# Selective scan in a four-block kernel: VectorE's products with B in pairs of units, GpSimd's two products at the end of a step

## The chip, the cores and the metric

One NeuronCore of a Trainium2 chip runs the whole program. The metric is the device time of one execution in microseconds (us), the median of several runs. All data are float32.

## The reference, cut to what matters

The program applies four blocks to an image tensor of 4 x 96 channels x 64 x 64. The change lies in the last, a selective scan in four directions (k = 0 to 3) over the 4096 pixels of each of 4 images, with 16 states per channel:

```python
def step(h, inp):
    u_t, d_t, B_t, C_t = inp
    h = jnp.exp(d_t[..., None] * A) * h + (d_t * u_t)[..., None] * B_t[:, :, None, :]
    y = jnp.einsum('bkdn,bkn->bkd', h, C_t)
    return (h, y)
_, ys = jax.lax.scan(step, h0, seq)
```

The product in question is `(d_t * u_t) * B_t`: one value of `d*u` per channel and pixel, times one value of B per state and pixel. It is the second summand of the recurrence.

## The kernel before, in words

The scan stage (`selective_scan`) works on **steps**. A step is one chunk of 512 pixels of one direction of one image; 4 images x 4 directions x 8 chunks make 128 steps, numbered n. Each step has 12 **units** (G = 12): 8 channels x 16 states fill the 128 partitions, 512 pixels lie along the free axis. For unit i of a step:

- PE copies delta to the unit's 128 rows with a matmul into one of three PSUM buffers (`replicate`, L1775, `p_da`, DAS = 3). It waits until the scan of unit i-3 has freed its buffer.
- ACT turns it into the decay by an Exp in place (`decay`, L1920).
- SP has brought `d*u`, repeated for the 16 states, by a DMA from a DRAM scratch into one of 8 ring slots in SBUF (`replicate_du`, L1698, `du_rep`, RING = 8). Slot (12 par + i) mod 8 is overwritten when the unit that used it has been multiplied. `par` is n mod 2.
- VectorE multiplies it with B, which lies in PSUM (`times_b`, L2054, `bu`, BUS = 3 buffers). For two units of a step, i = 5 and i = 11 (`ON_POOL`), GpSimd does this from a copy of B in SBUF (`times_b`, L2008, `pool_bu`), and issues it 4 units ahead of its own loop (BU_AHEAD): before its products with C of units 1 and 7.
- VectorE runs the recurrence along the 512 pixels (`scan`, L2069, into `h[:, i]`). Except in the first chunk of a direction (c = 0) it starts from the last state of the step before, read from `h`.
- GpSimd multiplies `h` with C (`times_c`, L2015, `hc`, a ring of 8), and PE sums over the states, three units at a time (`y_triple`, L1783).

Beside this each step carries the preparation of the next steps. It is written out by hand as positions between the units of each engine's loop, and the engines meet by counting semaphores only. What matters here:

- **PE**: `replicate(0)`, y_triple of the last step, `replicate(1)`, `b_mm(n+1)` (L1750), `replicate(2)`, `low_mm` (L1770, L1771), `replicate(3)`, y_triple, `replicate(4)`, `y_whole` (L1796), `replicate(5)`, `dt_mm(n+2)` (L1736), `replicate(6)`, `y_triple(n, 0)`, `replicate(7)`, `replicate(8)`, `c_mm(n+1)` (L1745), `replicate(9)`, `y_triple(n, 1)`, `replicate(10)`, first half of `delta_sum(n+2)` (L1759, L1760), `replicate(11)`, second half (L1762, L1765), and `replicate(0)` of the next step. The first half of `delta_sum` writes the PSUM tile out of which ACT's `c_copy(n+1)` reads, and waits for that copy.
- **ACT**: after `decay(5)` `take_y` (L1931), after `decay(6)` two activations (L1866, L1867), after `decay(7)` L1871, after `decay(8)` L1875 and L1879, after `decay(9)` L1882 and `c_copy(n+1)` (L1916), after `decay(10)` `b_copy(n+1)` (L1909, which waits until GpSimd has done its last product with B of step n), then `decay(11)`, and `decay(0)` of the next step, then two activations of `delta_and_high` (L1889, L1891).
- **GpSimd**: `times_c` in order of units, its two `times_b`, and `delta_u(n+1)` (L1997) before `times_c(2)`.
- **SP**: `replicate_du` of units 8 to 11 of step n, `restack(n+1)` (four DMAs, L1672), `store_du(n+1)` (L1683), `replicate_du` of units 0 to 7 of step n+1; each waits for the product that frees its slot, in this order.
- **VectorE**: `times_b(i+1)`, then `scan(i)`; where i+1 is one of GpSimd's units the product is left out, so two scans stand together. At i = 11 it is the product of unit 0 of the next step, which waits for `b_copy`.

Of the kernel before, what the change touches and what calls it, by code (L numbers as in the profile page):

```python
# [15 lines left out]
ALU = mybir.AluOpType  # L16
# [10 lines left out]
N = 512  # L27
# [1493 lines left out]
def selective_scan(nc, w, X, du_d):  # L1521
    K, S, R, DL = 4, 16, 6, 8
    G = C // DL
# [6 lines left out]
    TRIPLES = G // YT  # L1530
    HCS = 8
    DAS = 3
    BUS = 3
    RING = 8
    ON_POOL = (5, 11)
    BU_AHEAD = 4
    NB = G - len(ON_POOL)
    COLS = N // H
    GRP = [(i % YT) * YJ + i // YT for i in range(G)]
    with ExitStack() as ctx:  # L1540
# [28 lines left out]
        du_rep = sb("l3_du_rep", [128, RING, N])  # L1569
        c_rep = sb("l3_c_rep", [128, 2, N])  # L1570
        bu = sb("l3_bu", [128, BUS, N])
        h = sb("l3_h", [128, G, N])
        hc = sb("l3_hc", [128, HCS, N])
        b_sb = sb("l3_b_sb", [128, N])
        pool_bu = sb("l3_pool_bu", [128, len(ON_POOL), N])
        pick_f = hc[0:C].rearrange("c a n -> c (a n)")[:, 0:Q // DL * 128].rearrange("c (j p) -> c j p", p=128)

        p_da = [ps(f"l3_p_da{i}", [128, N]) for i in range(DAS)]
        p_b = [ps(f"l3_p_b{i}", [128, N]) for i in range(2)]
# [12 lines left out]
        s_dur = [sem(f"l3_du_replicated{i}") for i in range(RING)]  # L1592
        s_c, s_ccp, s_b = sem("l3_c_mm"), sem("l3_c_copied"), sem("l3_b_mm")
        s_rep, s_da, s_bu, s_h, s_hc, s_ymm, s_ysum, s_y = (sem("l3_" + n) for n in (
            "delta_replicated", "da", "bu", "h", "hc", "y_triple", "y_whole", "y_taken"))

        H0, HC0, YMM0, Y0, HI0, LO0, CCP0, DU0, DUS0, BU0, PBU0 = DAS, G, TRIPLES, 2, 1, 1, 1, 1, 16, 2 * NB, 2 * len(ON_POOL)
        weights = [(xp_dt, "xp_dt"), (dt_w, "dt_w_T"), (w_rep, "w_rep"), (pick_f, "pick"),
# [46 lines left out]
        def ring_at(par, i):  # L1645

            return (G * par + i) % RING

        def ring_count(n, par, i):

            return 16 * (G // 4 * (n - par) // (RING // 4) + (G * par + i) // RING) + 16

        def vector_bus(i):

            return sum(j not in ON_POOL for j in range(i))

        def stacked_by(m, par):

# [2 lines left out]
        @block.sync  # L1661
        def _(sp_):
            for dst, src in weights:
                sp_.dma_start(dst[:], w[src]).then_inc(s_w, 16)

            def restack(m, par):

                sp_.wait_ge(s_lo, m + 1 + LO0)
                sp_.nop(nofuse=True)
                for part in range(2):  # L1670
                    for q in range(PARTS):
                        sp_.dma_start(stacked[part * Q:(part + 1) * Q, par, q].bitcast(F32),  # L1672
                                      parts[q * Q:(q + 1) * Q, part].bitcast(F32)).then_inc(s_stack[par], 16)

            def store_du(m, par):

                sp_.wait_ge(s_du, m + 1 + DU0)
                sp_.nop(nofuse=True)
                sp_.wait_ge(s_bu, NB * (m - 1) + BU0)
                sp_.nop(nofuse=True)  # L1680
                sp_.wait_ge(s_pbu, len(ON_POOL) * (m - 1) + PBU0)
                sp_.nop(nofuse=True)
                sp_.dma_start(du_d[par], du[:]).then_inc(s_dus, 16)  # L1683

            def replicate_du(n, par, i):

                if i == 0:
                    sp_.wait_ge(s_dus, 16 * (n + 1) + DUS0)
                    sp_.nop(nofuse=True)
                user, step_of = (i - RING) % G, (i - RING) // G  # L1690
                if user in ON_POOL:
                    sp_.wait_ge(s_pbu, len(ON_POOL) * (n + step_of) + ON_POOL.index(user) + 1 + PBU0)
                else:
                    sp_.wait_ge(s_bu, NB * (n + step_of) + vector_bus(user) + 1 + BU0)
                sp_.nop(nofuse=True)
                src = du_d[par, GRP[i] * DL:(GRP[i] + 1) * DL]
                src = bass.AP(src.tensor, src.offset, [[0, S], [N, DL], [1, N]])
                sp_.dma_start(du_rep[:, ring_at(par, i)], src).then_inc(s_dur[ring_at(par, i)], 16)  # L1698

            def step(n, par, more):  # L1700
                for i in range(RING, G):
                    replicate_du(n, par, i)
                if more:
                    sp_.wait_ge(s_rep, G * n)
                    sp_.nop(nofuse=True)
                    restack(n + 1, 1 - par)
                    store_du(n + 1, 1 - par)
                    for i in range(RING):
                        replicate_du(n + 1, 1 - par, i)

            store_du(0, 0)
            restack(0, 0)
            for i in range(RING):
                replicate_du(0, 0, i)
            step(0, 0, True)
            with sp_.Fori(0, B * STEPS // 2 - 1) as i:
                step(2 * i + 1, 1, True)
                step(2 * i + 2, 0, True)
            step(B * STEPS - 1, 1, False)

        @block.tensor
        def _(pe):
# [24 lines left out]
            def b_mm(m, par, b, k, c):  # L1747
                pe.wait_ge(s_bu, NB * (m - 1) + BU0)
                pe.nop(nofuse=True)
                pe.matmul(p_b[par][:], w_rep[:, k, 0, :], u_of(b, k, c), start=True, stop=True).then_inc(s_b, 1)  # L1750
# [280 lines left out]
        @block.vector  # L2031
        def _(dve):
            dve.wait_ge(s_setup, K)
            dve.tensor_copy(w_dt[:].rearrange("c k d -> c (k d)"), p_bc[0:C, 0:K * C]).then_inc(s_setup_cp, 1)
            dve.wait_ge(s_w, 16 * len(weights))
            dve.tensor_copy(pick[:], pick_f[:]).then_inc(s_setup_cp, 1)
            dve.tensor_scalar(minus[:], ident[:], -1.0, None, ALU.mult).then_inc(s_setup_cp, 1)
            dve.tensor_scalar(minus_r[:], ident[:], -1.0, None, ALU.mult).then_inc(s_setup_cp, 1)
            dve.tensor_reduce(d_sum[:], cols[:, K:2 * K], AX_X, ALU.add).then_inc(s_setup_cp, 1)
            dve.memset(ln_one[:], 1.0).then_inc(s_setup_cp, 1)  # L2040
            dve.wait_ge(s_a, 2)
            dve.tensor_scalar(a_neg[:], a_neg[:], -1.0, None, ALU.mult).then_inc(s_a, 1)
            dve.tensor_scalar(ln_one[:], ln_one[:], -1.0, None, ALU.mult).then_inc(s_a, 1)
            dve.wait_ge(s_setup_cp, 6)
            dve.tensor_scalar(d_diag[:], ident[:], d_sum[:], None, ALU.mult).then_inc(s_setup_cp, 1)
            for s, credit in ((s_bu, BU0), (s_h, H0), (s_dus, DUS0)):
                dve.sem_inc(s, credit)

            def times_b(n, i, par):
                if i == 0:  # L2050
                    dve.wait_ge(s_bcp, n + 1)
                dve.wait_ge(s_dur[ring_at(par, i)], ring_count(n, par, i))
                dve.wait_ge(s_h, G * n + i + 1 - BUS + H0)
                dve.tensor_tensor(bu[:, i % BUS, :], du_rep[:, ring_at(par, i)], p_b[par][:], ALU.mult).then_inc(s_bu, 1)  # L2054

            def scan(n, k, c, i, par):
                backward = k >= 2
                way = slice(None, None, -1) if backward else slice(None)
                first = 0 if backward else N - 1
                dve.wait_ge(s_da, G * n + i + 1)  # L2060
                dve.wait_ge(s_hc, G * (n - 1) + i + 1 + HC0)
                if i in ON_POOL:
                    dve.wait_ge(s_pbu, len(ON_POOL) * n + ON_POOL.index(i) + 1 + PBU0)
                    of = pool_bu[:, ON_POOL.index(i), way]
                else:
                    dve.wait_ge(s_bu, NB * n + vector_bus(i) + 1 + BU0)
                    of = bu[:, i % BUS, way]
                state = 0.0 if isinstance(c, int) and c == 0 else h[:, i, first:first + 1]
                dve.tensor_tensor_scan(h[:, i, way], p_da[i % DAS][:, way], of, state, ALU.mult, ALU.add).then_inc(s_h, 1)  # L2069

            def step(b, n, k, c, par, n1, n2, before):
                for i in range(G):
                    if i < G - 1 and i + 1 not in ON_POOL:
                        times_b(n, i + 1, par)
                    if i == G - 1 and n1:
                        times_b(n + 1, 0, 1 - par)
                    scan(n, k, c, i, par)

            times_b(0, 0, 0)
            all_steps(step)(dve)  # L2080
            dve.wait_ge(s_y, B * STEPS + Y0)

# [201 lines left out]
```

## Time and profile before

| | us |
|---|---|
| median of 3 runs (lowest, highest) | 5742.23 (5741.26, 5752.42) |
| the profiled execution: its own time | 5744.95 |
| its span in the trace | 5743.1 |
| first scan of the scan stage starts | 3070.7 |
| last scan starts | 5653.8 |
| VectorE busy over the span | 4640.4 (81%) |
| PE busy | 4971.3 (87%) |
| GpSimd busy | 3832.2 (67%) |
| ACT busy | 2949.7 (51%) |

The span runs from the first to the last recorded instruction. Busy time is the sum of the records of an engine; on VectorE and ACT the record of an instruction overlaps the start of the next by some 0.09 us when they follow without a gap, so the time that an instruction takes out of a busy engine is read from start to start, not from its record. The scan stage takes 45% of the span, and the change touches only that stage.

### The profile page before, as it was taken

To read this page: it belongs to the slowest core of one execution; us is meant where nothing else is said; L and a number is where in the kernel's file an instruction comes from. 1 tells how busy PE (TensorE), PEld (TensorE's weight loads), DVE (VectorE), ACT (ScalarE), POOL (GpSimd) and SP (SyncE) were. 2 spreads that over 40 slices of the span, in tenths; PEclk is the share of its full clock that TensorE was granted. 3 is DMA by queue.
4 is the path that set the end of the run, shared out by engine and by line. 5 is a ranking of instruction groups with operands and counts; after the bars stand their busy time and mean duration, and the time that the engine had idled before them with its cause. 6 is when DMAs were issued, how large, how long until landed. Compare 5 with 4: busy or idle time off the path is not lost. (4 is left out here: it accounts for less than half of the span.)

```text
span 5743.1 us, 74310 instructions
## 1 busy us (share of the span) xinstructions
PE 4971.3 (87%) x16018; PEld 2207.8 (38%) x16018; DVE 4640.4 (81%) x5047; ACT 2949.7 (51%) x4576; POOL 3832.2 (67%) x2568
## 2 busy tenths in 40 slices
PE   6999889897779999998297888888888888888887
PEld 1222256464256666665152222222222222222222
DVE  4876643434418989899797999999999999999996
ACT  5776544443311111111135777777777777777776
POOL 0000032322418898888786999989998999999993
PEclk9998899998889999998698999999999999999998
DMA  2000000001777787776405667667766666677663
GB/s 47 0 0 0 7 1 1 0 1 56 226 158 139 138 152 140 147 141 107 91 9 138 185 183 189 185 182 189 187 186 178 186 185 187 184 189 189 187 184 100
DMA packets 373418, 711.24 MB, mean 124 GB/s; under 512 B 76604, under 2 KB 111224, under 8 KB 358936
## 3 DMA queue, kind: packets, MB, share of 16 engines
q1 hardware_dynamic: 373144, 708.17, 50.2%
q8 instruction: 100, 1.64, 0.1%
q14 instruction: 174, 1.43, 0.1%
HBM read 575.33 MB, written 82.32 MB: 115 GB/s over the span
## 5 line engine op out<-in xcount | busy, mean ns | idle before, releaser
L2015 POOL TENSOR_TENSOR l_hc<-l_h,l_c_rep 128x512 f32<-128x512 f32 x1536 | 1929.8, 1276 | 216.0 <-DVE l_h L2069 187.1
L2069 DVE TENSOR_TENSOR_SCAN l_h<-l_p_da,l_h,l_bu 128x512 f32<-128x512 f32 x1120 | 1412.8, 1279 | 10.5 <-ACT l_p_da L1920 8.8
L1920 ACT ACTIVATE l_p_da<-l_p_da,l_a_neg 128x512 f32<-128x512 f32 x1536 | 1008.5, 658 | 733.8 <-PE l_p_da L1775 712.9
L1221 POOL TENSOR_TENSOR l2b_prod<-l2b_v,l2b_attn 128x1568 f32<-128x1568 f32 x276 | 937.3, 3461 | 242.9 <-DVE l2b_osum L1269 125.2
L1775 PE MATMUL l_p_da<-l_stacked,l_pick 96*128 96x512 f32 x1536 | 908.9, 593 | 191.3 <-DVE l_h L2069 179.1
L2054 DVE TENSOR_TENSOR l_bu<-l_du_rep,l_p_b 128x512 f32<-128x512 f32 x1280 | 855.7, 669 | 29.7 <-DMA l_du_rep<-du_scratch 22.5
L1775 PEld LDWEIGHTS l_p_da<-l_stacked,l_pick 96*128 96x128 f32 x1536 | 293.7, 192 | 1162.4 <-DVE l_h L2069 900.3
L1269 DVE TENSOR_REDUCE l2b_osum<-l2b_prod 128x32 f32<-128x1568 f32 x384 | 665.7, 1780 | 62.9 <-POOL l2b_prod L1221 59.2
L1783 PE MATMUL l_p_y<-l_hc,l_y_pick 128*32 128x512 f32 x3072 | 566.4, 626 | 74.3 <-POOL l_hc L2015 71.7
L1174 ACT ACTIVATE l2b_logits<-l2b_conv,l2b_this_b 98x512 f32<-98x512 f32 x96 | 66.2, 689 | 870.5 <-PE l2b_conv L1139 870.5
L615 POOL TENSOR_TENSOR l_w_pos_low<-l1a_w_sed,l_w_pos_high 96x1536 fp32r<-96x1536 f32 x1 | 4.1, 4123 | 711.2 <-DVE l_w_fc_high L595 711.2
L1139 PE MATMUL l2b_conv<-l2b_img_high,l2b_w_conv_high 128*98 128x512 f32 x1344 | 358.8, 420 | 38.7 <-DMA l2b_img_low<-qkv_scratch 38.7
L1139 PE MATMUL l2b_conv<-l2b_img_high,l2b_w_conv_low 128*98 128x512 f32 x1344 | 338.8, 403 | 0.0
L1139 PE MATMUL l2b_conv<-l2b_img_low,l2b_w_conv_high 128*98 128x512 f32 x1344 | 337.3, 402 | 0.0
L2008 POOL TENSOR_TENSOR l_pool_bu<-l_du_rep,l_b_sb 128x512 f32<-128x512 f32 x256 | 326.7, 1276 | 0.0
L1139 PEld LDWEIGHTS l2b_conv<-l2b_img_high,l2b_w_conv_high 128*98 128x98 f32 x1344 | 231.7, 174 | 148.4 <-issue 38.1
L2069 DVE TENSOR_TENSOR_SCAN l_h<-l_p_da,l_h,l_pool_bu 128x512 f32<-128x512 f32 x224 | 287.4, 1283 | 1.3 <-ACT l_p_da L1920 1.0
L770 POOL TENSOR_TENSOR l1b_h_h_low<-l1b_h_h,l1b_h_h_high 128x512 fp32r<-128x512 f32 x96 | 125.6, 1320 | 226.2 <-DVE l1b_h_h_high L734 226.2
L1139 PEld LDWEIGHTS l2b_conv<-l2b_img_high,l2b_w_conv_low 128*98 128x98 f32 x1344 | 219.6, 163 | 103.9
L1139 PEld LDWEIGHTS l2b_conv<-l2b_img_low,l2b_w_conv_high 128*98 128x98 f32 x1344 | 219.6, 163 | 102.3
L1759 PE MATMUL l_p_bc<-l_relu_x,l_ident 96*96 96x512 f32 x256 | 144.6, 648 | 66.5 <-ACT l_c_rep L1916 59.3
L2069 DVE TENSOR_TENSOR_SCAN l_h<-l_p_da,l_bu 128x512 f32<-128x512 f32 x160 | 192.6, 1222 | 7.7 <-ACT l_p_da L1920 7.6
(267 smaller groups left out, 8905.2 us busy)
## 6 DMA issues: line engine op xcount, KB each, us to landing
l_du_rep<-du_scratch SPq DMA_DIRECT2D x1536, 256.0 KB, 3.8
l2b_img_high<-qkv_scratch SPq DMA_DIRECT2D x192, 306.2 KB, 5.6
l2b_img_low<-qkv_scratch SPq DMA_DIRECT2D x192, 306.2 KB, 9.4
l_stacked<-l_parts SPq DMA_DIRECT2D x512, 96.0 KB, 2.7
l2b_v<-v_scratch SPq DMA_DIRECT2D x192, 152.0 KB, 6.4
qkv_scratch<-l2a_strip SPq DMA_DIRECT2D x32, 840.0 KB, 5.2
du_scratch<-l_du SPq DMA_DIRECT2D x128, 192.0 KB, 2.1
v_scratch<-l2a_v_strip SPq DMA_DIRECT2D x32, 228.0 KB, 4.2
```

The costliest lines, as they stand in the source:

```text
L770: pool.tensor_tensor(h_hl[1][:, f, :], h[:, f, :], h_hl[0][:, f, :], ALU.subtract).then_inc(s_h_lo, 1)
L1139: mm = pe.matmul(p_conv[n % 2][:], w_conv[w_part][:, g, dx, :], img[x_part][:, b % 2, row:row + 2 * CP - 1:2, dx:dx + W], start=(at == 0), ...
L1221: return eng.tensor_tensor(dst.rearrange("q x (dy dx) -> q x dy dx", dx=WIN), window, attn_half[:, :, unit % 2].rearrange("q x (dy dx) -> ...
L1269: dve.tensor_reduce(osum[:, half, unit // 2, unit % 2, :], prod[which][:], AX_X, ALU.add).then_inc(s_sum, 1)
L1759: pe.matmul(p_bc[0:C, :], ident[:], relu_x[:], start=True, stop=False)
L1775: pe.matmul(p_da[i % DAS][:], pick[:, GRP[i] % (Q // DL), :], stacked[:, par, GRP[i] * DL // Q, :], start=True, stop=True).then_inc(s_rep, 1)
L1783: mm = pe.matmul(p_y[par][q * 32:(q + 1) * 32, :], y_pick[:, t, :], hc[:, (G * par + YT * t + q) % HCS, :], start=(t == 0), stop=False)
L1920: act.activation(p_da[i % DAS][:], p_da[i % DAS][:], ACT.Exp, scale=a_neg[:, k * G + GRP[i]:k * G + GRP[i] + 1]).then_inc(s_da, 1)
L2008: pool.tensor_tensor(pool_bu[:, at, :], du_rep[:, ring_at(par, i)], b_sb[:], ALU.mult).then_inc(s_pbu, 1)
L2015: pool.tensor_tensor(hc[:, (G * par + i) % HCS, :], h[:, i, :], c_rep[:, par, :], ALU.mult).then_inc(s_hc, 1)
L2054: dve.tensor_tensor(bu[:, i % BUS, :], du_rep[:, ring_at(par, i)], p_b[par][:], ALU.mult).then_inc(s_bu, 1)
L2069: dve.tensor_tensor_scan(h[:, i, way], p_da[i % DAS][:, way], of, state, ALU.mult, ALU.add).then_inc(s_h, 1)
```

## The change

VectorE's ten products with B of a step become five instructions, each for two units next to each other (0 and 1, 2 and 3, up to 8 and 9). An instruction reads two ring slots of `du_rep` (1024 elements), reads B's 512 columns of PSUM twice by a step of zero, and writes two of now four `bu` buffers. It waits for the DMAs of both units. GpSimd's two units are now 10 and 11 instead of 5 and 11. VectorE's loop changes its order: `scan(i)` comes first, behind it, for even i up to 6, the pair (i+2, i+3), and behind `scan(10)` the pair (0, 1) of the next step. So a step's order is scan 0, pair (2, 3), scan 1, scan 2, pair (4, 5), scan 3, scan 4, pair (6, 7), scan 5, scan 6, pair (8, 9), scan 7, scan 8, scan 9, scan 10, pair (0, 1) of n+1, scan 11. GpSimd issues its two products before its products with C of units 6 and 7. SP's waits for a free ring slot now count pairs.

```diff
-    BUS = 3
+    BUS = 4
-    ON_POOL = (5, 11)
+    ON_POOL = (10, 11)
-    NB = G - len(ON_POOL)
+    NB = (G - len(ON_POOL)) // 2
...
+        def bu_at(par, i):
+            return (2 * NB * par + i) % BUS
...
-                    sp_.wait_ge(s_bu, NB * (n + step_of) + vector_bus(user) + 1 + BU0)
+                    sp_.wait_ge(s_bu, NB * (n + step_of) + user // 2 + 1 + BU0)
...
             def times_b(n, i, par):
                 if i == 0:
                     dve.wait_ge(s_bcp, n + 1)
-                dve.wait_ge(s_dur[ring_at(par, i)], ring_count(n, par, i))
-                dve.wait_ge(s_h, G * n + i + 1 - BUS + H0)
-                dve.tensor_tensor(bu[:, i % BUS, :], du_rep[:, ring_at(par, i)], p_b[par][:], ALU.mult).then_inc(s_bu, 1)
+                for j in (i, i + 1):
+                    dve.wait_ge(s_dur[ring_at(par, j)], ring_count(n, par, j))
+                user = i + 1 - BUS if i >= BUS else i + 1 + 2 * NB - BUS - G
+                if user >= 0 or not (isinstance(n, int) and n == 0):
+                    dve.wait_ge(s_h, G * n + user + 1 + H0)
+                both = p_b[par][:]
+                both = bass.AP(both.tensor, both.offset, [list(both.ap)[0], [0, 2], [1, N]])
+                at = bu_at(par, i)
+                dve.tensor_tensor(bu[:, at:at + 2, :], du_rep[:, ring_at(par, i):ring_at(par, i) + 2, :],
+                                  both, ALU.mult).then_inc(s_bu, 1)
...
-                    dve.wait_ge(s_bu, NB * n + vector_bus(i) + 1 + BU0)
-                    of = bu[:, i % BUS, way]
+                    dve.wait_ge(s_bu, NB * n + i // 2 + 1 + BU0)
+                    of = bu[:, bu_at(par, i), way]
...
             def step(b, n, k, c, par, n1, n2, before):
                 for i in range(G):
-                    if i < G - 1 and i + 1 not in ON_POOL:
-                        times_b(n, i + 1, par)
-                    if i == G - 1 and n1:
+                    scan(n, k, c, i, par)
+                    if i % 2 == 0 and i + 2 < 2 * NB:
+                        times_b(n, i + 2, par)
+                    if i == G - 2 and n1:
                         times_b(n + 1, 0, 1 - par)
-                    scan(n, k, c, i, par)
```

## Rows read from the trace of the kernel before

**Rows 1.** Page, costliest groups: busy us, mean ns | idle before, releaser.
```profile
L2015 POOL TENSOR_TENSOR l_hc<-l_h,l_c_rep 128x512 f32<-128x512 f32 x1536 | 1929.8, 1276 | 216.0 <-DVE l_h L2069 187.1
L2069 DVE TENSOR_TENSOR_SCAN l_h<-l_p_da,l_h,l_bu 128x512 f32<-128x512 f32 x1120 | 1412.8, 1279 | 10.5 <-ACT l_p_da L1920 8.8
...
L2054 DVE TENSOR_TENSOR l_bu<-l_du_rep,l_p_b 128x512 f32<-128x512 f32 x1280 | 855.7, 669 | 29.7 <-DMA l_du_rep<-du_scratch 22.5
```

**Rows 2.** Windows: busy (x) of PE, PEld, DVE, ACT, POOL, clock, DMA share, GB/s.
```profile
4000.00:4500.00 500.00, 435.38 (x1354) 142.64 (x1353) 490.98 (x541) 357.52 (x597) 457.16 (x368) 0.98 0.69 184
```

**Rows 3.** VectorE's timeline, one step from its scan 0 (4953.73) to the next: start, duration.
```profile
4953.73 1.30 DVE L2069 TENSOR_TENSOR_SCAN l_h<-l_p_da,l_h,l_bu 128x512 f32<-128x512 f32 x1
4954.92 0.68 DVE L2054 TENSOR_TENSOR l_bu<-l_du_rep,l_p_b 128x512 f32<-128x512 f32 x1
4955.50 1.30 DVE L2069 TENSOR_TENSOR_SCAN l_h<-l_p_da,l_h,l_bu 128x512 f32<-128x512 f32 x1
...
4961.99 1.30 DVE L2069 TENSOR_TENSOR_SCAN l_h<-l_p_da,l_h,l_pool_bu 128x512 f32<-128x512 f32 x1
...
4973.80 1.29 DVE L2069 TENSOR_TENSOR_SCAN l_h<-l_p_da,l_h,l_bu 128x512 f32<-128x512 f32 x1
```

**Rows 4.** VectorE's timeline in a first chunk (c = 0).
```profile
4533.44 1.23 DVE L2069 TENSOR_TENSOR_SCAN l_h<-l_p_da,l_bu 128x512 f32<-128x512 f32 x1
4534.57 0.67 DVE L2054 TENSOR_TENSOR l_bu<-l_du_rep,l_p_b 128x512 f32<-128x512 f32 x1
```

**Rows 5.** VectorE's groups by form, other blocks: larger element-wise products and sums.
```profile
L1221 DVE TENSOR_TENSOR l2b_prod<-l2b_p_v,l2b_attn 128x1568 f32<-128x1568 f32 x108 | 191.8, 1776 | 0.7
...
L345 DVE TENSOR_TENSOR l_dt<-l_gain 96x1024 f32<-96x1024 f32 x32 | 38.7, 1211 | 0.0
...
L347 DVE TENSOR_TENSOR l_gain<-l_dt 96x512 f32<-96x512 f32 x32 | 22.0, 687 | 1.1
```

**Rows 6.** PE's timeline, the same step as rows 3 (L1775: units 4, 8, 0 of the next).
```profile
4956.85 0.50 PE L1775 MATMUL l_p_da<-l_stacked,l_pick 96*128 96x512 f32 x1 [0.24 <-DVE l_h L2069]
...
4963.35 0.50 PE L1775 MATMUL l_p_da<-l_stacked,l_pick 96*128 96x512 f32 x1 [0.40 <-DVE l_h L2069]
...
4967.77 1.07 PE L1759 MATMUL l_p_bc<-l_relu_x,l_ident 96*96 96x512 f32 x2 [0.38 <-ACT l_c_rep L1916]
...
4971.08 0.80 PE L1775 MATMUL l_p_da<-l_stacked,l_pick 96*128 96x512 f32 x1
```

**Rows 7.** ACT's timeline, the same step (L1920: units 4, 8, 0 of the next).
```profile
4957.39 0.66 ACT L1920 ACTIVATE l_p_da<-l_p_da,l_a_neg 128x512 f32<-128x512 f32 x1 [0.56 <-PE l_p_da L1775]
...
4964.09 0.64 ACT L1920 ACTIVATE l_p_da<-l_p_da,l_a_neg 128x512 f32<-128x512 f32 x1
...
4971.91 0.66 ACT L1920 ACTIVATE l_p_da<-l_p_da,l_a_neg 128x512 f32<-128x512 f32 x1 [1.29 <-PE l_p_da L1775]
```

**Rows 8.** Two scans that waited for their decay: ACT's and VectorE's timelines.
```profile
4549.03 0.66 ACT L1920 ACTIVATE l_p_da<-l_p_da,l_a_neg 128x512 f32<-128x512 f32 x1 [1.39 <-PE l_p_da L1775]
...
4549.90 1.23 DVE L2069 TENSOR_TENSOR_SCAN l_h<-l_p_da,l_pool_bu 128x512 f32<-128x512 f32 x1 [0.44 <-ACT l_p_da L1920]
...
5173.98 0.66 ACT L1920 ACTIVATE l_p_da<-l_p_da,l_a_neg 128x512 f32<-128x512 f32 x1 [1.29 <-PE l_p_da L1775]
...
5174.67 1.22 DVE L2069 TENSOR_TENSOR_SCAN l_h<-l_p_da,l_bu 128x512 f32<-128x512 f32 x1
```

**Rows 9.** Who waited for the decay tile l_p_da: us in all, times.
```profile
  DVE l_h L2069: 20.9, 17
```

**Rows 10.** GpSimd's timeline, the same step as rows 3.
```profile
4955.19 1.28 POOL L2015 TENSOR_TENSOR l_hc<-l_h,l_c_rep 128x512 f32<-128x512 f32 x1 [0.51 <-DVE l_h L2069]
4956.44 1.27 POOL L2008 TENSOR_TENSOR l_pool_bu<-l_du_rep,l_b_sb 128x512 f32<-128x512 f32 x1
```

**Rows 11.** The DMA queue's timeline of that step, and issue to landing of l_du_rep.
```profile
4963.29 11.21 SPq L1698 DMA_DIRECT2D l_du_rep<-du_scratch  x10
...
DMA to landing us min/median/max: 3.0/3.8/6.8
```

More of the change, by code:

```diff
@@ L1647, in ring_at @@
             return (G * par + i) % RING
+        def bu_at(par, i):
+            return (2 * NB * par + i) % BUS
         def ring_count(n, par, i):
             return 16 * (G // 4 * (n - par) // (RING // 4) + (G * par + i) // RING) + 16
-        def vector_bus(i):
-            return sum(j not in ON_POOL for j in range(i))
         def stacked_by(m, par):
```

## The prediction

> **What bounds the kernel now.** I read the costliest groups first [rows 1]: in the scan stage VectorE runs 1536 scans (the row has 1120 of them) of 1.28 us and 1280 products of 0.67 us, and both groups have next to no idle time before them. The stage's windows come next [rows 2]: of 500 us VectorE is busy 491, PE 435, GpSimd 457, ACT 358. So VectorE ends the stage, but PE and GpSimd have little to spare. Then one step on VectorE [rows 3]: from product to scan it is 0.58 us, from scan to the next instruction 1.19 us, start to start. The step holds ten products and twelve scans, 10 x 0.58 + 12 x 1.19 = 20.08 us, and the row shows 4973.80 - 4953.73 = 20.07. There is no gap in it. In a first chunk a scan takes 1.13 [rows 4], so such a step would need 5.80 + 13.56 = 19.36. There are 16 first chunks and 112 others.
>
> **The pairs, on VectorE alone.** A step loses ten products of 0.58 and gets five of 1024 elements. No row shows a product that reads PSUM twice by a step of zero. Nearest are element-wise rows of other blocks [rows 5]: 512 elements 687 ns, 1024 elements 1211 ns, so 512 more elements cost 0.524; and a product out of PSUM with a windowed pattern, 1568 elements in 1776 ns, against 669 for 512 [rows 1], which is 1.048 ns per element, 0.537 for 512. A pair then takes 0.58 + 0.524 to 0.537 = 1.104 to 1.117 start to start; by its whole record less the usual overlap of 0.09 it would be 1.12. I take 1.115, nearest to the row that reads PSUM. Two singles are 1.16, so a pair saves 0.045 us (0.04 to 0.056), a step 0.225, the stage 128 x 0.225 = 28.8 us (25.6 to 35.8). The new order puts no scan and no pair right behind the instruction whose result it needs, so I add nothing for that; five added waits for DMAs are taken by the sequencer while the engine works, at nothing as the old ones are now. What remains of the saving depends on who is late next.
>
> The Trainium skill (Vector Engine (DVE) Microarchitecture Reference, section on the rate slope and fixed cost) gives 1.0417 ns per column plus about 75 ns per instruction after overlap; the trace has 0.58 - 0.533 = 0.045 us here, so it does not agree in size. By the page the saving would be an estimated 128 x 5 x 0.075 = 48 us.
>
> **The chain behind VectorE.** The scan of unit i needs its decay, that needs PE's replicate, and that needs the scan of i-3. Between them PE and ACT do the preparation. The tight place is around the step's end. Scan 5 starts at 4961.99 [rows 3]; replicate(8) starts 1.36 later at 4963.35 [rows 6]. From a replicate to its decay, where ACT is free, it is 4957.39 - 4956.85 = 0.54 [rows 6, 7]. From decay(8) at 4964.09 to decay(0) of the next step at 4971.91 it is 7.82 [rows 7]: ACT runs its activations without a gap up to c_copy, which releases PE's L1759 [rows 6], and four delta_sum products and two replicates follow on PE without a gap. From the start of a decay to the scan that waits for it the trace has 0.87 and 0.69 [rows 8]. Today scan 0 starts 4973.80 - 4971.91 = 1.89 after its decay, so it has 1.02 us to spare.
>
> After the change more of VectorE's work stands ahead of scan 5 and less behind it. Scan 5 starts 5 x 1.19 + 3 x 1.115 = 9.30 us into the step (now 8.26). Behind it VectorE alone has 7 x 1.19 + 2 x 1.115 = 10.56 us to the next scan 0; the chain has 1.36 + 0.54 + 7.82 + 0.69 to 0.87 = 10.41 to 10.59. So **VectorE alone gives a step of 19.86, the chain 19.71 to 19.89**: a tie. I take 19.87, a gain of 0.205, and 112 such steps give 23.0 us. In a first chunk scan 5 starts at 5 x 1.13 + 3 x 1.115 = 9.00, its record is 0.06 shorter, and the chain ends at 9.00 + 10.35 to 10.53 = 19.35 to 19.53, against 19.14 for VectorE and 19.36 now: 16 steps lose 0 to 0.17, I take 1.6 us in all.
>
> **What the lost slack costs.** Today a scan waits for its decay 17 times, 20.9 us in all [rows 9]. The granted clock in the stage averages 0.98 [rows 2], so for a small part of it PE runs at the lower of its two levels, 1.2 instead of 2.4 GHz, and a step in which this meets the chain starts up to 1.02 us late without a trace today. With no slack left each of the 17 waits can grow by 1.0 (17 us), and hidden ones show; some shrink, since early delays on ACT now end before decay(8). Between 0 and 17 I take 8.
>
> **Edits that I cost at nothing, and their cover.** GpSimd: product follows product by 1.25 us [rows 10], so its 15 operations of a step take 18.6 of 19.9. Its product for unit 5 no longer stands ahead of times_c(1). Counted on from scan 5 (times_c follows a scan's start by 4955.19 - 4953.73 = 1.46 us where it waits [rows 3, 10]), it does times_c(5) at 10.8, the product for 10 at 12.0, times_c(6) at 13.2, the product for 11 at 14.5 to 15.8. VectorE needs the first at scan 10, at 16.4, the second at 18.7. ACT's b_copy waits for the second and would run 15.9 to 16.5; decay(11) behind it waits for PE until some 17.0 anyway, and the pair (0, 1) of the next step needs b_copy at 17.6. Both have about 1 us. SP: the ten issues before the next step's need take 11.21 us and land in 3.8 (6.8 at most) [rows 11]. The slots of the pair (0, 1) are written from 9.6 us into the step and now are both needed at 17.6 (unit 0 at 19.5 before), land at 14 to 17; replicate_du(10) waits for the whole pair (2, 3), some 1.2 us into the step plus 1.1, and restack behind it moves by up to 1 us, of the 10 that it is early. ACT's other decays keep 0.7 us (unit 11) or more. Nothing here ends last, but all of it is closer.
>
> **Sum.** -23.0 + 1.6 + 8 = -13.4 us. The profiled execution took 5744.95, so 5731.6 against its own time; the median of the runs is 2.7 lower, 5742.23 - 13.4 = **5729 us**. 0.2% is 11.5 us, about what a measurement of this kernel can tell from no change: faster means below 5730.7, slower above 5753.7.
>
> **Rivals.**
> 1. VectorE alone counts: the wake-up is 0.69 in most steps, delays stay rare, or the pair is cheaper than the rows say. For it: nearly every step of rows 3's kind has no gap. Against it: the chain ends within 0.03 us of VectorE's own. With the full 28.8 us the time is 5713, with 0.056 saved by a pair 5706. Chance 0.18.
> 2. The part of a product that does not grow with its length is larger than the rows say, and a pair saves 0.075 us, taking 1.085. VectorE alone would then need 14.28 + 5.43 = 19.71 per step, the chain 5.95 + 3.26 + 10.41 to 10.59 = 19.62 to 19.80. Steps of 19.71 to 19.80 gain 0.27 to 0.36 each, 35 to 46 us; less 8 for the delays that is 5704 to 5715. Against it: 0.58 start to start for 512 elements leaves no such part. Chance 0.04. (The fixed cost of the page named above is this case.)
> 3. The chain holds the stage: a link is 0.15 us longer than I read it, at PE (L1759 right behind replicate(10), which now starts near 14.1 us) or ACT. Each 0.1 us costs 12.8 us; 0.15 with the delays gives -13.4 + 19 = 5748, within 0.2%. For it: there is no slack to absorb a link. Against it: all links are taken from one gapless stretch. With the gain merely halved by delays (17 us instead of 8) it is 5738. Chance of the group 0.22.
> 4. **Slower**: GpSimd's late second product. It decides from the point where the product for unit 11 ends over 1.0 us later than counted (16.8 us into the step instead of 15.8): then b_copy is late, the pair (0, 1) waits, and decay(11) and delta_sum's results queue behind b_copy on ACT. Each 0.1 us beyond it costs 12.8 us; 0.3 beyond it, with the gain of 13 gone as well from the lengthened step (20.17), gives 5742 + 12 + 8 = 5762. For it: both products now lie between times_c(5) and times_c(7), in the busiest part of GpSimd's step. Against it: GpSimd still stands idle for 0.51 us at the step's start [rows 10], so it catches up there. Chance 0.07.
>
> **How the numbers follow.** My forecast (5717 to 5738) has 0.49, the four rivals 0.18, 0.04, 0.22 and 0.07. Faster by over 0.2% are rivals 1 and 2 and about six tenths of the forecast's range, since 5730.7 cuts it just above its middle: 0.53. Same: the rest of it and rival 3: 0.40. Slower: 0.07. The range goes from 5708 (near rival 1 with 0.056 saved by a pair) to 5744 (rival 3's larger part), leaving out half of rival 2 and the slower case.
>
> **What the profile after would show.** Right: 640 products of 128x1024 with a record near 1.20 us and 1.11 to 1.12 to the next start; steps of 19.85 to 19.9; scan 0 starting 0.7 to 0.9 behind decay(0), where it was 1.89; the count of scans that wait for ACT well above 17, mostly at unit 0 and in first chunks; GpSimd busier per step. Wrong: a pair start to start at 1.16 or above (the broadcast read of PSUM costs), steps of 20 us with the wait at unit 0 (rival 3), products waiting for ACT's b_copy or for a DMA (rival 4), or steps well under 19.8 (rival 2).

## The result, and the profile after

The changed kernel takes 5809.51 us (median of 4, 5805.63 to 5818.54); the kernel before, with one more run taken beside it, 5745.77 (4 runs). The ratio is 1.0112, 95% interval 1.0095 to 1.0130: slower by 64 us, where 13 us less were forecast. The time lies far above the stated range.

The page's groups of the scan stage after the change, against [rows 1] (busy us, mean ns | idle before, releaser):

```profile
L2015 POOL TENSOR_TENSOR l_hc<-l_h,l_c_rep 128x512 f32<-128x512 f32 x1536 | 1922.1, 1273 | 292.0 <-DVE l_h L2076 269.2
L2076 DVE TENSOR_TENSOR_SCAN l_h<-l_p_da,l_h,l_bu 128x512 f32<-128x512 f32 x1120 | 1374.7, 1269 | 60.1 <-ACT l_p_da L1920 58.5
...
L1775 PE MATMUL l_p_da<-l_stacked,l_pick 96*128 96x512 f32 x1536 | 1023.0, 666 | 274.0 <-DVE l_h L2076 266.9
...
L2060 DVE TENSOR_TENSOR l_bu<-l_du_rep,l_p_b 128x1024 f32<-128x1024 f32 x640 | 765.9, 1197 | 25.7 <-DMA l_du_rep<-du_scratch 23.3
```

VectorE did get cheaper: 640 pairs of 1.20 us are 766 us, where 1280 products were 856. But the scans now stand idle before they start, for ACT's decay, and PE's replicate takes 666 ns on average. Before it was 593:

```profile
L1775 PE MATMUL l_p_da<-l_stacked,l_pick 96*128 96x512 f32 x1536 | 908.9, 593 | 191.3 <-DVE l_h L2069 179.1
```

The windows show why, against [rows 2]; the columns are the same, the third number from the end is the granted clock:

```profile
4000.00:4500.00 500.00, 439.93 (x1310) 148.00 (x1307) 471.78 (x405) 349.96 (x579) 442.00 (x357) 0.91 0.67 178
```

The clock of TensorE was 0.98 of 2.4 GHz in this window and is 0.91. Counted over the trace from the first scan to the last, PE stood at 1.2 GHz for 511 us in 95 stretches, against 138 us in 26 before. First to last scan start is 3075.3 to 5725.1 = 2649.8 us, where it was 2583.1: 67 us more. Outside the stage the profiled executions differ by 7 us.

Two neighbouring steps make it plain, the first at full clock, the second with a fall. Each is one window, which begins some 0.5 us behind the step's scan 0:

```profile
3634.40:3654.20 19.80, 17.15 (x56) 5.74 (x55) 19.77 (x18) 14.51 (x25) 18.49 (x16) 1.00 0.72 189
3654.20:3675.90 21.70, 20.14 (x57) 6.76 (x56) 20.09 (x18) 14.63 (x25) 19.86 (x17) 0.84 0.71 186
```

From scan 0 to scan 0 the first step takes 3653.73 - 3633.84 = 19.89 us, the second 3675.40 - 3653.73 = 21.67. PE's timeline inside the second:

```profile
3661.28 1.06 PE L1783 MATMUL l_p_y<-l_hc,l_y_pick 128*32 128x512 f32 x6
3662.27 0.50 PE L1775 MATMUL l_p_da<-l_stacked,l_pick 96*128 96x512 f32 x1
3664.34 0.79 PE L1775 MATMUL l_p_da<-l_stacked,l_pick 96*128 96x512 f32 x1 [1.56 <-DVE l_h L2076]
3664.93 1.91 PE L1745 MATMUL l_p_bc<-l_xt,l_w_rep 96*128 x2
...
3667.19 1.93 PE L1783 MATMUL l_p_y<-l_hc,l_y_pick 128*32 128x512 f32 x6
3669.05 0.80 PE L1775 MATMUL l_p_da<-l_stacked,l_pick 96*128 96x512 f32 x1
3669.65 1.77 PE L1759 MATMUL l_p_bc<-l_relu_x,l_ident 96*96 96x512 f32 x2
```

PE has done replicate(7) at 3662.8 and then has nothing to do for 1.56 us, until scan 5 is over. In [rows 6] this wait was 0.40. When replicate(8) starts, the clock has fallen (the trace has the lower level from 3664.33 to 3671.16): a y_triple takes 1.93 instead of 1.06 us, c_mm 1.91 instead of 1.02. VectorE's timeline shows the bill at the end of that step:

```profile
3670.77 1.28 DVE L2076 TENSOR_TENSOR_SCAN l_h<-l_p_da,l_h,l_pool_bu 128x512 f32<-128x512 f32 x1 [0.66 <-POOL l_hc L2015]
...
3673.42 1.28 DVE L2076 TENSOR_TENSOR_SCAN l_h<-l_p_da,l_h,l_pool_bu 128x512 f32<-128x512 f32 x1 [0.25 <-ACT l_p_da L1920]
3675.40 1.28 DVE L2076 TENSOR_TENSOR_SCAN l_h<-l_p_da,l_h,l_bu 128x512 f32<-128x512 f32 x1 [0.70 <-ACT l_p_da L1920]
```

These are scans 10, 11 and the next 0. Their idle times add up to 1.6 us; the step is 1.78 us longer than the one before it, since a record overlaps the next by some 0.1 us where nothing waits. The first is put down to GpSimd, but decay(10) on ACT started 0.88 before it, the distance of [rows 8]: it too waited for its decay.

```profile
3669.89 0.66 ACT L1920 ACTIVATE l_p_da<-l_p_da,l_a_neg 128x512 f32<-128x512 f32 x1 [0.90 <-PE l_p_da L1775]
```

All in all, who waited on VectorE after 3100 us (us in all, times, longest):

```profile
DVE l_h L2076 <- ACT l_p_da L1920: 93.8, 135, 4.3
DVE l_h L2076 <- POOL l_hc L2015: 15.0, 23, 0.7
```

That is 109 us in 158 waits, against 20.9 us in 17 waits in [rows 9].

### The profile page after: what moved, and what is told of

Same layout as the page of the kernel before. It is cut to its first block and busy times, and to the rows that moved or that the text cites. A ratio compares the mean times of both kernels' runs of the same rounds, so it can differ in the third digit from the quotient of the medians.

```text
span 5816.7 us, 73352 instructions
## 1 busy us (share of the span) xinstructions
PE 5070.4 (87%) x16018; PEld 2254.5 (39%) x16018; DVE 4617.1 (79%) x4407; ACT 2965.2 (51%) x4576; POOL 3826.1 (66%) x2568
## 5 line engine op out<-in xcount | busy, mean ns | idle before, releaser
L2076 DVE TENSOR_TENSOR_SCAN l_h<-l_p_da,l_h,l_bu 128x512 f32<-128x512 f32 x1120 | 1374.7, 1269 | 60.1 <-ACT l_p_da L1920 58.5
L1920 ACT ACTIVATE l_p_da<-l_p_da,l_a_neg 128x512 f32<-128x512 f32 x1536 | 1013.1, 661 | 765.2 <-PE l_p_da L1775 748.7
L1775 PE MATMUL l_p_da<-l_stacked,l_pick 96*128 96x512 f32 x1536 | 1023.0, 666 | 274.0 <-DVE l_h L2076 266.9
L2060 DVE TENSOR_TENSOR l_bu<-l_du_rep,l_p_b 128x1024 f32<-128x1024 f32 x640 | 765.9, 1197 | 25.7 <-DMA l_du_rep<-du_scratch 23.3
L1775 PEld LDWEIGHTS l_p_da<-l_stacked,l_pick 96*128 96x128 f32 x1536 | 311.7, 203 | 1210.4 <-DVE l_h L2076 1055.5
L1783 PE MATMUL l_p_y<-l_hc,l_y_pick 128*32 128x512 f32 x3072 | 620.9, 683 | 8.9 <-POOL l_hc L2015 4.9
L1221 DVE TENSOR_TENSOR l2b_prod<-l2b_p_v,l2b_attn 128x1568 f32<-128x1568 f32 x108 | 191.8, 1776 | 0.7
```

The source lines that it names most:

```text
L1221: return eng.tensor_tensor(dst.rearrange("q x (dy dx) -> q x dy dx", dx=WIN), window, attn_half[:, :, unit % 2].rearrange("q x (dy dx) -> ...
L1775: pe.matmul(p_da[i % DAS][:], pick[:, GRP[i] % (Q // DL), :], stacked[:, par, GRP[i] * DL // Q, :], start=True, stop=True).then_inc(s_rep, 1)
L1783: mm = pe.matmul(p_y[par][q * 32:(q + 1) * 32, :], y_pick[:, t, :], hc[:, (G * par + YT * t + q) % HCS, :], start=(t == 0), stop=False)
L1920: act.activation(p_da[i % DAS][:], p_da[i % DAS][:], ACT.Exp, scale=a_neg[:, k * G + GRP[i]:k * G + GRP[i] + 1]).then_inc(s_da, 1)
L2060: dve.tensor_tensor(bu[:, at:at + 2, :], du_rep[:, ring_at(par, i):ring_at(par, i) + 2, :], both, ALU.mult).then_inc(s_bu, 1)
```

## The experiments

Theory A: the new order opens a gap in PE's work, the clock falls behind it, and PE at 1.2 GHz stretches the chain to scan 0, which has no slack. The rivals are named with each run. "Gap" is PE's idle time ahead of replicate(8) in one step. The clock and the steps are those of the profiled execution; "steps" leaves out first chunks and a few that were held up otherwise.

| kernel | us (median) | ratio to before (95%) | clock, 4000 to 4500 us | steps |
|---|---|---|---|---|
| changed | 5809.5 | 1.0112 (1.0095 to 1.0130) | 0.91 | 19.89; with a fall 20.2 or 21.7 |
| a_fill | 5722.1 | 0.9958 (0.9942 to 0.9975) | 0.99 | 19.88 |
| a_two_singles | 5856.4 | 1.0199 (1.0182 to 1.0216) | 0.90 | 20.1 to 22.3 |
| b_pool_late | 5814.0 | 1.0114 (1.0094 to 1.0134) | 0.90 | 20.1 to 23.2 |
| b_hole | 5843.4 | 1.0185 (1.0144 to 1.0226) | 0.90 | 20.1 to 22.0 |
| b_pool_late_fill | 5758.5 | 1.0023 (1.0010 to 1.0036) | 0.96 | 20.08; with a fall 20.3 |
| a_early | 5776.4 | 1.0059 (1.0035 to 1.0084) | 0.91 | 19.8 to 22.0 |
| a_fill_early | 5700.6 | 0.9920 (0.9895 to 0.9946) | 0.99 | 19.76 |
| a_spread_early | 5754.8 | 1.0014 (1.0000 to 1.0029) | 0.93 | 19.78 to 21.2 |
| b_fill_early | 5737.7 | 0.9981 (0.9969 to 0.9994) | 0.98 | 20.08 |

**a_fill: the gap filled.** In the changed kernel:

```diff
-                pe.matmul(p_da[i % DAS][:], ...).then_inc(s_rep, 1)
+                for _ in range({7: 3}.get(i, 1)):
+                    mm = pe.matmul(p_da[i % DAS][:], ...)
+                mm.then_inc(s_rep, 1)
```

> The changed kernel with the matmul of replicate(7) issued three times instead of once (it starts its PSUM tile anew each time, so the result is the same); PE is then busy for some 0.7 us more of the 1.56 us in which it stood idle before replicate(8). Theory A (the changed order opens a gap on PE behind unit 7, after which the granted clock falls to its lower level, and PE at 1.2 GHz stretches a chain that has no slack): the stage's mean clock goes from 0.90 back to 0.97 or above, most steps take 19.88 us, and the time is 5715 to 5740. Theory B (the lost slack alone makes the time, the clock falls for reasons of its own): added PE work helps nothing, clock 0.90, 5805 to 5830.

5722.1 us, 87 less than the changed kernel and 24 less than the kernel before. PE's timeline:

```profile
4005.08 0.95 PE L1776 MATMUL l_p_da<-l_stacked,l_pick 96*128 96x512 f32 x3
4007.14 0.50 PE L1776 MATMUL l_p_da<-l_stacked,l_pick 96*128 96x512 f32 x1 [1.11 <-DVE l_h L2078]
4007.47 1.02 PE L1745 MATMUL l_p_bc<-l_xt,l_w_rep 96*128 96x512 f32 x2
```

Two useless matmuls make replicate(7) 0.45 us longer; the gap that is left is 1.11 us, and the clock stays up: 42 us at the lower level in the stage, in 5 stretches, instead of 511 in 95. Theory A holds, theory B falls. VectorE's work, its order and its slack are those of the changed kernel.

**a_two_singles: the pairs undone, their place kept.**

```diff
-                dve.tensor_tensor(bu[:, at:at + 2, :], du_rep[:, ring_at(par, i):ring_at(par, i) + 2, :], both, ALU.mult).then_inc(s_bu, 1)
+                dve.tensor_tensor(bu[:, at, :], du_rep[:, ring_at(par, i)], p_b[par][:], ALU.mult)
+                dve.tensor_tensor(bu[:, at + 1, :], du_rep[:, ring_at(par, i + 1)], p_b[par][:], ALU.mult).then_inc(s_bu, 1)
```

> The changed kernel, but each pair is issued as two products of 512 elements one behind the other, at the same place and with the same waits. Theory A (gap on PE, clock): the order and the gap stay, so the clock falls as often, and with 0.22 us more per step on VectorE the time is 5810 to 5850, clock near 0.90. Rival C (the product of 1024 elements with its repeated read of PSUM disturbs PE or ACT): the clock recovers and the time is near 5745. Rival D (the step's length and its phase, 19.88 against 20.08, is what makes the clock fall): the clock is as in the kernel before, 0.97.

5856.4, a little above what A gave, with the clock at 0.90. VectorE alone needs 20.08 us a step again here, as in the kernel before, and the shortest steps take that. So neither the long instruction (C) nor the step's length (D) makes the clock fall. The order and GpSimd's place remain.

**b_pool_late: one line of the change, in the kernel before.**

```diff
-    ON_POOL = (5, 11)
+    ON_POOL = (10, 11)
```

> The kernel before with only GpSimd's two units moved from 5 and 11 to 10 and 11; singles and the old order stay. Theory A: scan 5 gets later by one product (0.58 us) while VectorE's total stays 20.08; no lump of work stands ahead of scan 5, so the gap on PE ahead of replicate(8) grows little, from 0.4 to 0.6 us or so, the slack of decay(0) falls from 1.0 to some 0.4 us; 5745 to 5765. If moving GpSimd's products were the cause of the loss (rival: GpSimd late, b_copy waits), 5800 or more.

5814.0: this line alone costs 68 us. I had expected 5745 to 5765. I had priced the wait ahead of replicate(8) at 0.6 us; it is 1.28 us, since scan 5 comes 0.58 later while replicate(7) also ends earlier, its y_triple no longer waiting for GpSimd. First the kernel before, then this one:

```profile
4961.46 1.06 PE L1783 MATMUL l_p_y<-l_hc,l_y_pick 128*32 128x512 f32 x6 [0.56 <-POOL l_hc L2015]
4962.45 0.49 PE L1775 MATMUL l_p_da<-l_stacked,l_pick 96*128 96x512 f32 x1
...
3999.18 1.06 PE L1783 MATMUL l_p_y<-l_hc,l_y_pick 128*32 128x512 f32 x6
4000.32 0.49 PE L1775 MATMUL l_p_da<-l_stacked,l_pick 96*128 96x512 f32 x1
4002.10 0.50 PE L1775 MATMUL l_p_da<-l_stacked,l_pick 96*128 96x512 f32 x1 [1.28 <-DVE l_h L2069]
```

Its expectation gave 5800 or more to the rival that GpSimd's products are late, so this run alone does not decide between gap and GpSimd; b_pool_late_fill below does.

**b_hole: a gap made on PE alone, in the kernel before.**

```diff
-                    if i == 6:
-                        y_triple(n, 0, par)
...
                     if n1 and i == 8:
                         c_mm(n + 1, *n1, n2)
+                    if i == 8:
+                        y_triple(n, 0, par)
```

> The kernel before with one edit on PE alone: y_triple(n, 0) comes behind c_mm at unit 8 instead of behind replicate(6), so 1.06 us of PE work leaves the stretch between replicate(6) and replicate(8); VectorE, ACT and GpSimd keep their order and there is 1.0 us of slack in the chain. Theory A: the clock falls in a large part of the steps, as in the changed kernel (mean of the stage 0.90 to 0.93), with a smaller loss since the slack of 1.0 us is still there: 5750 to 5790. Theory B: no change of the clock, 5740 to 5750.

5843.4, more than the 5750 to 5790 expected, with a clock of 0.90. VectorE, ACT and GpSimd run the old order here. Moving 1.06 us of PE's work out of the stretch before replicate(8) is enough to bring the clock down. The steps without a fall still take 20.08, so the moved y_triple costs nothing at full clock. With a fall it stands in the chain ahead of replicate(9) at half speed. That is the likely reason why b_hole costs more than the changed kernel; no run tests it by itself:

```profile
4002.39 0.50 PE L1775 MATMUL l_p_da<-l_stacked,l_pick 96*128 96x512 f32 x1 [0.67 <-DVE l_h L2069]
4004.16 0.79 PE L1775 MATMUL l_p_da<-l_stacked,l_pick 96*128 96x512 f32 x1 [1.28 <-DVE l_h L2069]
4004.75 1.91 PE L1745 MATMUL l_p_bc<-l_xt,l_w_rep 96*128 x2
4006.59 1.93 PE L1783 MATMUL l_p_y<-l_hc,l_y_pick 128*32 128x512 f32 x6
```

**b_pool_late_fill: b_pool_late with replicate(7) three times.**

> The kernel before with GpSimd's units moved to 10 and 11, and replicate(7) issued three times. Theory A (the gap on PE in front of replicate(8), 1.27 us in b_pool_late, makes the clock fall): the stage's mean clock returns to 0.97 or above and the time to 5740 to 5755, since the steps without a fall were 20.08 there. Theory E (GpSimd's products at 10 and 11, or b_copy behind them, cost time of their own): 5780 or more even at the higher clock.

5758.5 us, 3.5 us above the top of what A gave, and 56 below b_pool_late. The clock is 0.96, where A gave 0.97 or above; PE is at the lower level for 196 us in 49 stretches, instead of 535 us in 105. The steps without a fall are 20.08, so GpSimd's new place costs the stage nothing by itself (theory E falls). Of the 13 us by which it is still slower than the kernel before, little is seen in the stage: the profiled executions differ by 16 us, of which the stage holds 4 (2586.9 against 2583.0) and the time ahead of its first scan 11 (3081.8 against 3070.7). Why that time differs is open.

The falls that remain also say something about theory A. Two steps of this run (replicate(7), (8), (9), then (8) and (9) of the next); the clock falls as replicate(9) runs, at 4008.76 and 4029.24:

```profile
4005.13 0.97 PE L1776 MATMUL l_p_da<-l_stacked,l_pick 96*128 96x512 f32 x3 [0.29 <-DVE l_h L2071]
4006.91 0.50 PE L1776 MATMUL l_p_da<-l_stacked,l_pick 96*128 96x512 f32 x1 [0.80 <-DVE l_h L2071]
4008.68 0.75 PE L1776 MATMUL l_p_da<-l_stacked,l_pick 96*128 96x512 f32 x1 [0.41 <-DVE l_h L2071]
...
4027.19 0.50 PE L1776 MATMUL l_p_da<-l_stacked,l_pick 96*128 96x512 f32 x1 [0.81 <-DVE l_h L2071]
4028.97 0.58 PE L1776 MATMUL l_p_da<-l_stacked,l_pick 96*128 96x512 f32 x1 [0.41 <-DVE l_h L2071]
```

The gap ahead of replicate(8) is 0.81 here with 49 falls, and it was 1.11 in a_fill with 5. So the length of this one gap does not decide alone. PE's other idle times around it differ too: here 0.41 follows ahead of replicate(9), in a_fill none does. Which measure of PE's work decides is not shown.

**a_early: slack given back, the gap kept.** On ACT:

```diff
+                    if n1 and i == 9:
+                        c_copy(n + 1, 1 - par)
                     if n2 and i == 9:
                         log_1e(n + 2)
-                    if n1 and i == 9:
-                        c_copy(n + 1, 1 - par)
```

> The changed kernel with ACT's c_copy put ahead of the activation L1882, so that PE's delta_sum can start 0.52 us earlier; the gap on PE stays. Theory A: the clock falls as often (mean 0.90 to 0.91), but each fall reaches a chain with 0.5 us of slack again: steps with a fall shorten by up to 0.5 us, 83 of them, so 5770 to 5800. Theory B (slack alone): the time is near that of the kernel with the gap filled, 5720 to 5740.

5776.4: 33 us less than the changed kernel, as A has it. The clock is still 0.91. Half a microsecond of slack wins back over a third of the 87 us that a_fill does; the falls go on, 104 of them.

**a_fill_early: both.**

> The changed kernel with both: replicate(7) three times, and c_copy ahead of L1882. With the clock kept up and 0.5 us of slack in the chain, VectorE alone sets the step. Theory A with the tie as predicted: a_fill had a median step of 19.88 with the wait at unit 0 in nearly every step; now 19.83 to 19.86, and first chunks 19.1 instead of 19.5, 5705 to 5720.

5700.6, 0.8% faster than the kernel before and below the 5705 to 5720 expected. VectorE's timeline has no gap in a step, from scan 0 at 4004.34 to the next at 4024.09, 19.75 us (second column: the record, of several scans together where it says so):

```profile
4003.14 1.27 DVE L2078 TENSOR_TENSOR_SCAN l_h<-l_p_da,l_h,l_pool_bu 128x512 f32<-128x512 f32 x1
4004.34 1.25 DVE L2078 TENSOR_TENSOR_SCAN l_h<-l_p_da,l_h,l_bu 128x512 f32<-128x512 f32 x1
4005.51 1.19 DVE L2062 TENSOR_TENSOR l_bu<-l_du_rep,l_p_b 128x1024 f32<-128x1024 f32 x1
4006.63 2.45 DVE L2078 TENSOR_TENSOR_SCAN l_h<-l_p_da,l_h,l_bu 128x512 f32<-128x512 f32 x2
4008.99 1.19 DVE L2062 TENSOR_TENSOR l_bu<-l_du_rep,l_p_b 128x1024 f32<-128x1024 f32 x1
...
4024.09 1.25 DVE L2078 TENSOR_TENSOR_SCAN l_h<-l_p_da,l_h,l_bu 128x512 f32<-128x512 f32 x1
```

I had given 19.83 to 19.86 for the step, by the pair price of the prediction; it is 19.76. A scan behind a pair takes 1.20 (4003.14 to 4004.34), one behind a scan 1.17 (4004.34 to 4005.51), a pair 1.12.

**a_spread_early: no work added, PE's own work moved into the gap.** In PE's loop `dt_mm(n+2)` stands at i = 6 instead of 5 and `y_triple(n, 0)` at i = 7 instead of 6, with a_early's edit beside it.

> The changed kernel with no added work, but PE's own work moved towards the gap: dt_mm(n+2) behind replicate(6) instead of replicate(5), y_triple(n, 0) behind replicate(7) instead of replicate(6), and c_copy ahead of L1882. Theory A: the idle time ahead of replicate(8) falls from 1.6 to some 0.5 us, but an idle stretch opens behind replicate(5); if the clock stays up (0.97), 5705 to 5735. If it falls in the new stretch, 5760 or more.

5754.8, between the two cases, and 22 us less than a_early, which has the same edit on ACT: the clock is 0.93, and it now falls at 7 us into the step instead of 11. The gap was moved, not closed; it lies behind replicate(5), ahead of replicate(6), seen here in two steps, the second with the fall:

```profile
4014.56 0.51 PE L1775 MATMUL l_p_da<-l_stacked,l_pick 96*128 96x512 f32 x1 [0.86 <-DVE l_h L2076]
4014.91 1.03 PE L1736 MATMUL l_p_bc<-x_back,l_w_dt 96*96 x2
...
4034.32 0.58 PE L1775 MATMUL l_p_da<-l_stacked,l_pick 96*128 96x512 f32 x1 [1.04 <-DVE l_h L2076]
4034.70 1.91 PE L1736 MATMUL l_p_bc<-x_back,l_w_dt 96*96 x2
```

**b_fill_early: the two helping edits without the change.** The kernel before, replicate(6) twice, c_copy early.

> The kernel before (singles, GpSimd's units 5 and 11) with replicate(6) issued twice and c_copy ahead of L1882: the two edits that help the changed kernel, without the change. The kernel before lost 27 us of its scan stage beyond 112 steps of 20.08 and 16 of 19.36, so these edits can give at most that: 5725 to 5746, and VectorE's step stays 20.08. If so, the pairs are worth the rest of the distance to a_fill_early (5701), 128 x 0.32 = 41 us by its step of 19.76. If this kernel comes near 5701 too, the pairs are worth nothing and the two edits did it all.

5737.7, 7.6 us less than before and inside the range expected. So the pairs with their new order are worth 5737.7 - 5700.6 = 37 us, close to the 41 that the steps give (20.08 against 19.76, 128 times), once the clock is held.

## Why the prediction was wrong

**What bounds, and VectorE's part: right in kind, a little low.** A pair takes 1.11 to 1.12 us start to start, where 1.115 was taken; the repeated read of PSUM costs nothing. The saving of a pair is 0.045, not the 0.075 that the Trainium skill (Vector Engine (DVE) Microarchitecture Reference, rate slope and fixed cost) would give: the trace does not agree with the page for this instruction. What the sum missed is that a scan takes 1.17 to 1.18 us where it follows a scan, not 1.19. Two of twelve do so in the old order, seven in the new. VectorE alone needs 19.76, not 19.86.

**The chain: right.** The forecast had replicate(8) at 10.66 us into the step, decay(0) at 19.02 and the step at 19.71 to 19.89. In steps at full clock they come at 10.61 and 18.98, and the step takes 19.89 (medians of the trace after). As VectorE needs only 19.76, it is no tie: nearly every scan 0 starts 0.13 us late, 1.31 behind scan 11 (3652.42 to 3653.73) where 1.17 to 1.18 would do. a_early's edit frees it.

**GpSimd, SP, the ring: right.** No pair waited for a DMA in the steady steps; b_copy waited for GpSimd 51 times, 20.9 us, and nobody queued behind it was late for that in a step at full clock.

**The step that failed is the price of the lost slack.** The prediction took the clock of the kernel before, 0.98, as given, and charged 8 us (17 at most) for its falls meeting a chain without slack. The number of falls was itself a result of the order of work: with the wait ahead of replicate(8) going from 0.4 to 1.56 us PE did too little there, and stretches at 1.2 GHz went from 26 to 95. Of the 95, 90 begin between 0.9 us before and 2.0 us behind the start of replicate(8). Counted over the trace without first chunks, 83 steps with a fall average 20.92 us and 28 without 20.05, where the 111 of before averaged 20.18: 83 x 0.74 - 28 x 0.13 = 58 us. A fall's price goes by its length: 44 steps with a stretch of 3.4 us at the lower level average 20.19, 37 with one of 6.8 us average 21.71. The 16 first chunks cost 8.5 us more in all; seven of them take 21.4 to 21.5 us, where those with nothing in the way take 19.5. The late end of the gap stood in the forecast, replicate(8) starting at 10.66; its early end, replicate(7), was not worked out. In the trace it is done 9.04 us into the step (3662.77 - 3653.73). I costed it at nothing, since PE's idle time is no wait of VectorE, and read no row for what PE's idle time does to PE's speed.

**With the clock held, the forecast of 5729 is the right size**: a_fill takes 5722. Outside first chunks its steps gain 25 us, where 23 were forecast; the 16 first chunks gain 5, where 1.6 us of loss were taken, and nothing of the 8 us for delays shows. The mechanism forecast (pairs, chain) is there; it was outweighed by one that was not among the rivals. The slower rival that was named, GpSimd's late product, is not the cause: a_fill has GpSimd's products in the same place and is fast, and the steps of b_pool_late_fill without a fall are as short as before.

## What to carry to other kernels

Before moving work on the bounding engine, write down where the other engines will stand idle, TensorE above all: in this kernel an idle stretch was paid for with the clock of the work behind it. Filling PE's gap and giving the last chain some slack was worth 109 us to the changed kernel (5809.5 to 5700.6), the saved instructions themselves 37. A repeated matmul that nobody waits for filled the gap; moving PE's own work into it opened another. And a gain in one engine's total is only as good as the slack of the chain that it takes it from.

## What the runs showed of the hardware

- In 93 of the 95 falls of the changed kernel's stage PE had not stood idle longer than 1.57 us in one piece in the 12 us before; the other two came behind 2.6 and 3.4 us. PE was busy 89% of the stage. In a_fill 0.45 us more of matmuls per step, with a gap of 1.11 us left, took the time at the lower level from 511 to 42 us; that so little decides was not expected. The Trainium skill (TensorE: Matmul & The Clock Gate, Part 1) says that activity releases a throttle that is otherwise on; the runs agree that PE's own work decides: a_fill and b_hole changed only that.
- The same operation at the two levels: y_triple 1.06 and 1.93 us, c_mm 1.02 and 1.91.
- A product of 1024 elements with a PSUM input read twice by a step of zero takes 1.197 us in the record, 0.53 more than one of 512 (0.669). That is 1.03 ns for each further element, and the rows without such a read gave 1.02 [rows 5].
